# Masking a causal attention on GpSimd and normalising it by 32x32 transposes; two of four expert lists built inside the expert loop

## What is computed

```
scores = jnp.einsum('bhqd,bhkd->bhqk', q, k) / math.sqrt(float(dh))
scores = jnp.where(causal, scores, -jnp.inf)
attn = jax.nn.softmax(scores, axis=-1)
o = jnp.einsum('bhqk,bhkd->bhqd', attn, v)
return o.transpose(0, 2, 1, 3).reshape(B, S, D) @ W_o.T
```

## Time and profile before

| | us |
|---|---|
| median of 3 runs | 686.37 (685.69 to 686.54) |
| the profiled execution | 689.58 |
| its span | 687.5 |
| busy: PE, DVE, ACT, POOL | 468.5, 451.6, 318.3, 249.7 |
| TensorE weight loads (beside PE) | 299.1 |
| mean granted TensorE clock, of full speed | 0.764 |

### The profile page before, as it was taken

One profiled execution on the slowest core, in us unless ns is written; L12 is line 12 of the kernel. 1 busy time (PEld: TensorE's weight loads), 2 busy tenths in 40 slices (PEclk: granted clock), 3 DMA queues, 4 the chain that ended last, 5 costly groups with the idle time before them and its releaser, 6 DMA issues.

```text
span 687.5 us, 10676 instructions
## 1 busy us (share of the span) xinstructions
PE 468.5 (68%) x3820; PEld 299.1 (44%) x3820; DVE 451.6 (66%) x778; ACT 318.3 (46%) x550; POOL 249.7 (36%) x380
## 2 busy tenths in 40 slices
PE   3956816567887997867787888877858137556540
PEld 2525703353555775655343333433337126434330
DVE  5897999968495767477888897988835861101003
ACT  1343305534203442457888888898842103333320
POOL 5443479972800000430111111111101045888870
PEclk9987867968998999898555555566557557999995
DMA  8630000000000000001999999999995165895546
GB/s 309 182 131 1 0 0 1 1 0 0 2 1 2 2 2 2 1 1 35 184 177 178 180 179 186 174 183 184 186 176 190 40 203 142 218 199 110 90 68 193
DMA packets 170259, 70.73 MB, mean 103 GB/s; under 512 B 142240, under 2 KB 167776, under 8 KB 170208
## 3 DMA queue, kind: packets, MB, share of 16 engines
q1 hardware_dynamic: 164064, 61.15, 41.8%
q0 software_dynamic: 6144, 8.92, 7.5%
HBM read 27.56 MB, written 8.93 MB: 53 GB/s over the span
## 4 chain that ended last, share of the span: by engine, by line
PE 28%; DVE 23%; issue 17%; ACT 12%; DMA 11%; POOL 8%; POOLq 0%; SPq 0%; DVEq 0%; ACTq 0%
ACT KV L610 8%; PE ps L662 5%; DMA KV<-KV 5%; DVE AT L1167 4%; POOL b L484 3%; DMA A<-x_rows,slot_token 3%; PE ps L816 3%; POOL sums L505 2%; PE ps L848 2%; ACT A L594 2%; DMA sums<-A,slot_token 2%; POOL A L491 2%; PE ps L831 2%; PE ps L654 2%; PE ps L829 1%
## 5 line engine op out<-in xcount | busy, mean ns | idle before, releaser
L1237 DVE TENSOR_REDUCE nm<-ps 128x1 f32<-128x1024 f32 x128 | 154.3, 1223 | 27.3 <-PE ps L894 25.6
L610 ACT ACTIVATE KV<-ps,b,sq 128x1024 int16<-128x1024 f32 x128 | 153.3, 1201 | 29.2 <-POOL b L484 14.7
L894 PE MATMUL ps<-A 128*128 128x512 bf16 x256 | 125.0, 590 | 34.7 <-ACT KV L610 32.8
L484 POOL TENSOR_SCALAR b<-nm,sq 128x1 f32<-128x1 f32 x128 | 33.8, 264 | 174.4 <-DVE nm L1237 148.9
L903 PEld LDWEIGHTS ps<-VI,KV 128*128 128x128 f16 x1024 | 55.0, 113 | 74.3 <-issue 53.4
L1326 DVE TENSOR_TENSOR AT<-AT,ps 128x128 f32<-128x128 f32 x32 | 9.2, 288 | 86.7 <-ACT AT L632 86.7
L505 POOL DMA_INDIRECT sums<-A,slot_token x32 | 50.8, 1586 | 21.5 <-ACT A L639 12.1
L903 PE MATMUL ps<-VI,KV 128*128 128x16 f16 x1024 | 50.9, 179 | 7.7 <-DMA KV<-KV 7.6
L413 POOL TENSOR_SCALAR veps<-mv 128x4 f32<-128x4 f32 x12 | 3.0, 248 | 142.6 <-DVE mv L981 142.5
L491 POOL DMA_INDIRECT A<-x_rows,slot_token x32 | 34.8, 1089 | 37.7 <-issue 35.9
L517 ACT ACTIVATE XT<-ps 128x256 f32<-128x256 f32 x48 | 18.3, 386 | 55.8 <-PE ps L654 55.7
(11 more groups left out here) (271 smaller groups left out, 1001.4 us busy)
## 6 DMA issues: line engine op xcount, KB each, us to landing
A<-in SPq DMA_DIRECT2D x32, 256.0 KB, 3.6
A<-in SPq DMA_DIRECT2D x32, 128.0 KB, 4.0
A<-in SPq DMA_DIRECT2D x2, 1024.0 KB, 14.2
sums<-zeros SPq DMA_DIRECT2D x4, 512.0 KB, 5.3
KV<-KV SPq DMA_TRANSPOSE x128, 3.3
A<-sums SPq DMA_DIRECT2D x8, 256.0 KB, 4.7
X<-in SPq DMA_DIRECT2D x1, 1024.0 KB, 6.0
ctxT<-in SPq DMA_DIRECT2D x1, 1024.0 KB, 8.6
```

Of the source, the lines that this page charges most:

```text
L484: g.tensor_scalar(b5[:, n % 4:n % 4 + 1], nm5[:, n % 4:n % 4 + 1], sq5[:, q, h:h + 1], LN255, ALU.mult, ALU.add).then_inc(S["bias5_ready"], 1)
L610: a.activation(Y5[:, n % 4, :], ps[:, 2 * (n % 3):2 * (n % 3) + 2, :], ACT.Exp, scale=sq5[:, q, h:h + 1], bias=b5[:, n % 4:n % 4 + 1], acc ...
L894: done = T.matmul(ps[:, 2 * (n % 3) + c, :], QT5[:, h, q * P:(q + 1) * P], KT5[:, h, c * 512:(c + 1) * 512], start=True, stop=True)
L1237: v.tensor_reduce(nm5[:, n % 4:n % 4 + 1], ps[:, 2 * (n % 3):2 * (n % 3) + 2, :].rearrange("p a c -> p (a c)"), AX.X, ALU.max, negate=True ...
```

## The change

1. **Mask.** The mask matmul (L829), causalT, its memset and its select go. The first matmul into a bank now has start=True. After the exponential POOL sets the entries above the diagonal of two heads to 0 (affine_select over 128 x 2 x 256 elements, in place, one per half group, 32 in all); O(u) waits for this (mask4_ready) and no longer for the exponential. The selects stand in POOL's order after vint_ready and ahead of norm_rstd(4).
2. **Sums.** V4 gets a column of ones at position 16 of each head; the matmuls with ones go. The sum of a query then lies on partition 32r + 16 of the head.
3. **Normalisation.** DVE transposes the 128x256 outcome in blocks of 32x32 from PSUM to SBUF, takes the reciprocal of 128x8 sums, multiplies 128x8x16, and transposes back into QT4. The bank is free after the first transpose.
4. **Lists.** Lists 0 and 1 are built ahead of the loop. Lists 2 and 3 are cut into three pieces each, at steps s = 0, 3, 6 and s = 8, 11, 14 of DVE's loop, and 3, 6, 11, 14 of PE's.

```diff
+LIST_AT = [0, 0, 0, 8]
-        causalT = sb("causalT", [P, P], BF16)
...
-        r4 = XT[:, :, :].rearrange("p k c -> p (k c)")[:, 1536:2048].rearrange("p (i c) -> p i c", i=2)
+        OQ4 = XT[:, :, :].rearrange("p k c -> p (k c)")[:, 1536:2048].rearrange("p (i n c) -> p i n c", i=2, c=32)
+        ON4 = A[:, 15360:15872].rearrange("p (i n c) -> p i n c", i=2, c=32)
+        r4 = sb("r4", [P, 2, 8])
...
-            g.memset(V4[:, :, :, HD:2 * HD], 0.0).then_inc(S["v4_pads"], 1)
+            g.memset(V4[:, :, :, HD:HD + 1], 1.0).then_inc(S["v4_pads"], 1)
+            g.memset(V4[:, :, :, HD + 1:2 * HD], 0.0).then_inc(S["v4_pads"], 1)
...
+            for n in range(2 * G4):
+                pool.wait_ge(S["exp4_ready"], n + 1)
+                e = E4[n // 2 % 3][:, 2 * (n % 2):2 * (n % 2) + 2, 0:2 * P].rearrange("p j (a c) -> p j a c", a=2)
+                g.affine_select(out=e, in_=e, compare_op=ALU.is_ge, fill=0.0, base=0,
+                                pattern=[[0, 2], [0, 2], [1, P]], channel_multiplier=-1).then_inc(S["mask4_ready"], 1)
             norm_rstd(4)
...
                     for r in range(4):
-                        T.matmul(ps[:, banks[r], 0:SEQ], identb[:, :], causalT[:, :].unsqueeze(1).to_broadcast([P, 2, P]), start=True, stop=True)
-                    for r in range(4):
-                        T.matmul(ps[:, banks[r], P:P + SEQ], k0[r], q01[r], start=False, stop=True, skip_group_check=True)
-                    for r in range(4):
-                        last = T.matmul(ps[:, banks[r], 0:P], k1[r], q1[r], start=False, stop=True, skip_group_check=True)
+                        T.matmul(ps[:, SETS4[(2 * i + r // 2) % 3] + r % 2, P:P + SEQ], k0[r], q01[r], start=True, stop=True)
+                    for r in range(4):
+                        last = T.matmul(ps[:, SETS4[(2 * i + r // 2) % 3] + r % 2, 0:P], k1[r], q1[r], start=True, stop=True)
...
-                    pe.wait_ge(S["exp4_ready"], 2 * u + 2)
+                    pe.wait_ge(S["mask4_ready"], 2 * u + 2)
...
+            v.memset(ON4[:, :, :, HD:32], 0.0).then_inc(S["on4_zero"], 1)
...
-                v.reciprocal(r4[:, u % 2, :], ps[:, bank, SEQ:2 * SEQ]).then_inc(S["r4_ready"], 1)
+                oq, on, r = OQ4[:, u % 2, :, :], ON4[:, u % 2, :, :], r4[:, u % 2, :]
+                v.transpose(oq.rearrange("p n c -> p (n c)"), ps[:, bank, 0:SEQ]).then_inc(S["oq4_ready"], 1)
+                dve.wait_ge(S["oq4_ready"], u + 1)
+                v.reciprocal(r, oq[:, :, HD]).then_inc(S["r4_ready"], 1)
                 dve.wait_ge(S["r4_ready"], u + 1)
-                v.tensor_tensor(QT4[:, g, b * SEQ:(b + 1) * SEQ], ps[:, bank, 0:SEQ], r4[:, u % 2, :], ALU.mult).then_inc(S["on4_ready"], 1)
+                v.tensor_tensor(on[:, :, 0:HD], oq[:, :, 0:HD], r.unsqueeze(2).to_broadcast([P, 8, HD]), ALU.mult).then_inc(S["om4_ready"], 1)
+                dve.wait_ge(S["om4_ready"], u + 1)
+                v.transpose(QT4[:, g, b * SEQ:(b + 1) * SEQ], on.rearrange("p n c -> p (n c)")).then_inc(S["on4_ready"], 1)
...
-            for n in range(NE // EG):
+            for n in range(2):
                 onehots(n)
+                list_diagonal(n)
                 tokens(n)
             for s in range(NE):
...
+                for n in range(2, NE // EG):
+                    if s == LIST_AT[n]:
+                        onehots(n)
+                    if s == LIST_AT[n] + 3:
+                        list_diagonal(n)
+                    if s == LIST_AT[n] + 6:
+                        tokens(n)
```

More of the change, by code:

```diff
@@ L378, in _ @@
             g.memset(onesb[:, :], 1.0).then_inc(S["const_ready"], 1)
-            g.memset(causalT[:, :], 0.0).then_inc(S["const_ready"], 1)
-            pool.wait_ge(S["const_ready"], 8)
+            pool.wait_ge(S["const_ready"], 7)
             for m in (identf, identb):
@@ L845, in _ @@
                     wait_o4_bank(pe, slot)
-                    for lo, w in ((0, [V4[:, 2 * b:2 * b + 2, 4 * g + r, :] for r in range(4)]), (SEQ, [onesf[:, 0:64].rearrange("p (t c) -> p t c", t=2)] * 4)):
-                        for r in range(4):
-                            T.matmul(ps[32 * r:32 * r + 32, bank, lo:lo + SEQ], w[r][:, 0, :], e[:, r, P:P + SEQ], start=True, stop=False)
-                        for r in range(4):
-                            last = T.matmul(ps[32 * r:32 * r + 32, bank, lo + P:lo + SEQ], w[r][:, 1, :], e[:, r, 0:P], start=False, stop=True)
+                    for r in range(4):
+                        T.matmul(ps[32 * r:32 * r + 32, bank, 0:SEQ], V4[:, 2 * b, 4 * g + r, :], e[:, r, P:P + SEQ], start=True, stop=False)
+                    for r in range(4):
+                        last = T.matmul(ps[32 * r:32 * r + 32, bank, P:SEQ], V4[:, 2 * b + 1, 4 * g + r, :], e[:, r, 0:P], start=False, stop=True)
                     last.then_inc(S["o4_psum"], 1)
@@ L935, in _, with list_spread @@
                 last.then_inc(S["grid_psum"], 1)
+            def list_spread(n):
                 pe.wait_ge(S["diag_ready"], n + 1)
                 T.matmul(ps[:, 7, n * 64:(n + 1) * 64], spread6[:, :], diag6[:, n % 2, :, :].rearrange("p e c -> p (e c)"), start=True, stop=True).then_inc(S["list_psum"], 1)
+            pe.wait_ge(S["const6_ready"], 4)
+            for n in range(2):
+                list_grid(n)
+                list_spread(n)
             for s in range(NE + 2):
```

20 lines of the change are left out of this document (11 added, 9 removed).

## The result

| | before | after | difference |
|---|---|---|---|
| median of the runs, us | 686.45 (4 runs) | 667.06 (4 runs) | -19.4, predicted -25.2 |
| ratio, 95% interval | | 0.970 (0.962 to 0.977) | |
| profiled execution, us | 689.58 | 669.24 | -20.3 |
| its span | 687.5 | 667.5 | -20.0 |
| busy PE, DVE, ACT, POOL | 468.5, 451.6, 318.3, 249.7 | 446.4, 441.1, 317.8, 271.6 | -22.1, -10.5, -0.5, +21.9 |

The forecast was 661.2 (656.5 to 668.5): the sign and the range held, and the median lies 5.9 us above the forecast. The narrower range that the prediction gave for its own account, 657.5 to 666, missed by 1.1 us.

The account below looks back on a forecast made before the run. It took PE's matmuls to bound pass 2, and POOL's scatters, started by PE's first expert, to bound the end. Gains of 19.9 (pass 2) and 5.3 us (lists) took 686.4 to 661.2 us, range 656.5 to 668.5.

Parts of the forecast that it names:

- the 19.9 of pass 2: Pass 2: without mask and ones matmuls its end moves from 281.8 to 261.9 us, a gain of 19.9 us.
- the 5.3 of the lists: Expert lists: two fewer ahead of the loop, less a new wait for the first gather, gain 5.3 us.
- rival 4: Expert lists: the work moved in delays POOL as much, so they give nothing; 666.5 us, chance 7%.
- rival 1: Pass 2: POOL's selects are the bound; at 2.14 us each 689.3 us, slower by 0.4%; chance 10%.
- The pace of pass 2: Pass 2: S, ACT's start, the exponential and PE's restart set a step of 1.86 us, not PE's own 1.66.
- they cost nothing up to 1.36 us each: Pass 2, POOL: four steps and an out_proj give 10.9 us for 8 selects, hiding up to 1.36 us each.
- I let it fall again: Early pass 2: PE's clock falls to 1.2 GHz at about 213 us and rises at 219.8, as before.
- the 5.2 us for the last out_proj: End of pass 2: the last out_proj takes 5.2 us, chosen between 3.65 and 6.71 at the low clock.
- Rival 2: Pass 2: PE's clock does not hold; 7 + 5 us are given back, 673 us; chance 8%.
- S(0) at 210.35 as now: Start of pass 2: the first S comes at 210.35 us, unchanged from the kernel before.
- The second memset in V4: Ahead of pass 2, POOL: the added memset is hidden, its results being wanted over 100 us later.
- rival 3: Pass 2, DVE: transpositions are slow; at 1.76 us each 692 us, slower; chance 5%.

Follow-up runs that it names:

- run 6: Changed kernel with masks by POOL's selects but the old normalisation (sums by matmuls with ones, reciprocal of 128x256 from PSUM): 677.35 us.
- run 7: Changed kernel with sums by V4 and normalisation by transpositions, but masks still written by matmuls: 674.92 us.
- run 9: Changed kernel with each select on POOL followed by one over half of its elements again: 669.26 us.
- run 8: Changed kernel with each select on POOL done twice in a row, with a wait between: 676.97 us.
- run 2: Changed kernel with the constant causalT made as before (one memset and one select more on POOL), though nothing reads it: 666.46 us.
- run 5: The kernel before the change once more, unaltered: 687.66 us, ratio 1.004 against other executions of the same kernel.
- run 4: Kernel before with only lists 2 and 3 moved into the expert loop, pass 2 and constants as before: 681.81 us, ratio 0.995.
- run 3: Changed kernel without its lists, all four built ahead of the expert loop as before: 671.08 us, ratio 0.979.
- run 10: Changed kernel with SP issuing the weights of experts 8 to 15 only after the first gather has landed: 665.00 us, ratio 0.973.

## Why the prediction was right, and where it was off

The two mechanisms that it named did what it said, and both terms of the sum can be found in the traces: 16.7 us at equal clock for the 19.9 of pass 2, and 5.6 for the 5.3 of the lists. The range held partly by luck: 667.06 is over the 666 up to which the forecast's own account went, and lies in the stated range only because that was widened for rival 4 and mild forms of rival 1, neither of which happened.

**The pace of pass 2: right.** The prediction put a step at 1.86 us, set by S, ACT's start, the exponential and PE's restart; it was 1.91, with PE waiting 0.19 for ACT. From S(4) to S(15) it had 30.8 us, and the trace 255.88 - 224.64 = 31.2. Runs 6 and 7 show that it is this loop: with the mask left on PE the step is 2.45, over PE's 2.20.

**The selects: cost right, slack wrong.** 0.69 us against 0.85 taken, and hidden but for 1.0 us at the last group. The sentence "they cost nothing up to 1.36 us each" failed. The tail may grow, which its range allowed for; but ahead of the tail, too, 0.8 us of the 1.3 were lost at 1.07 us a half group (run 9), and 5.2 of the 6.3 at 1.41, where the same average with the measured times would let POOL just keep up (run 8). It divided four steps and an out_proj by eight selects. In the middle of the pass that is nearly so (12.0 us a batch for 11.3 of selects). But the first out_proj comes only behind the seventh S, and until then POOL must keep the pace of a step, 1.91 / 2 = 0.95 us, or use up its lead of two groups; and in each batch it idles 0.76 us, since it can't work further ahead than S and the exponentials have got.

**DVE: right.** 0.445 us a transposition against 0.42 taken; a group 1.50 us from its first start to its last end (226.43 to 227.93) against 1.42, under the step of 1.91. The Trainium skill, "VectorE: DVE Perf Modes", section "The three transpose paths", led to an estimate of 0.62 us for this size. The trace does not agree: it is 0.445.

**Low clock in pass 2: wrong both ways.** The step "I let it fall again" cost the forecast 2.0 us (S(0) to S(4) 9.65 against 7.65 measured), and the 5.2 us for the last out_proj 1.7 (it took 3.5 until the keys started). Against that the tail and the steps were 0.7 longer. So the stretch came out 2.9 us shorter than forecast, 48.6 against 51.5. Rival 2 (the clock doesn't hold) did not come; PE waited 0.19 us in each step at 1.00. The Trainium skill, "TensorE: Matmul & The Clock Gate", section "A second HAM failure mode: psum-queue depth-cycling", had made it likely. None of the seven profiles with this pass 2 unaltered shows it: a granted clock of 1.00 in all of it, 48.6 to 49.0 us each.

**The base of the sum: the largest error.** The term of 19.9 us was 281.8 less 261.9, read against one profiled execution. That execution had its own luck with the clock: 5.6 us more in pass 2 than the two others of the same code, and a start of pass 2 at 210.35 where the others began at 213.80 and 207.69. At equal clock the gain in pass 2 is 16.7 us, 3.2 less than the term. The subtraction was right for that execution (22.7 measured, since the clock then did better than assumed) but not for the median of many. What lies ahead of pass 2 was taken to stay: "S(0) at 210.35 as now". It came at 216.99, and in no profile of the changed pass before 213.97.

**The second memset in V4: wrong, by all that the rows show.** The prediction held it hidden, "since POOL's results of that part are wanted over 100 us later". Its own results are, but DVE works beside it. Before the change and after it, the timeline of DVE:

```profile
92.72 4.00 DVE L988 TENSOR_SCALAR XN<-X,mv,rstd 128x256 f32<-128x256 f32 x4 [0.28 <-POOL rstd L415]
...
99.41 0.27 DVE L1090 TENSOR_SCALAR dq<-am,w 128x8 f32<-128x8 f32 x1
99.59 0.16 DVE L1092 TENSOR_SCALAR qs<-qs 128x8 f32<-128x8 f32 x1
```

```profile
92.71 4.29 DVE L1001 TENSOR_SCALAR XN<-X,mv,rstd 128x256 f32<-128x256 f32 x4 [0.28 <-POOL rstd L413]
...
99.80 0.59 DVE L1103 TENSOR_SCALAR dq<-am,w 128x8 f32<-128x8 f32 x1
100.31 0.16 DVE L1105 TENSOR_SCALAR qs<-qs 128x8 f32<-128x8 f32 x1
```

DVE's four passes beside the memsets take 4.29 us for 4.00 (the first alone 2.87 for 1.87, the others less than before), and behind them one small instruction takes 0.59 for 0.27. DVE reaches L1105 0.7 us later, and PE's first matmul of the feed-forward network comes as much later behind the same DVE pass in run 2 than in run 5. All three profiles with one memset have 4.00 (runs 4 and 5 and the first), and all eleven with two have 4.28 or 4.29 and 0.59 or 0.60. From the start of the first memset to DVE's L1092 or its counterpart pass 6.94 to 6.96 us in the three and 7.67 to 7.69 in the eleven, with the constants as before (run 2) or the lists as before (run 3) too. The Trainium skill, "SBUF — State Buffer", section "SBUF: two separate sides", says that POOL and some of DVE's instructions shut each other out for whole instructions rather than share. That would give steps of this kind, and no run here takes it apart. That the split of the memset is the cause is read from these rows; no run puts the single memset back alone.

**What stays open.** In three profiles with the old memset the first S of pass 2 comes at 207.69 to 213.80, in all eleven with the new at 213.97 to 217.16. Means are 4.8 us apart: 0.8 are there already when that memset starts (90.4 to 92.7 us in the three, 91.1 to 93.4 in the eleven); 0.7 are the memset's; 1.3 come in the feed-forward network up to V's projection; and 2.0 from there on. The constants are excluded (run 2). The last part is one level of the clock: V's projection took 4.64 us in two of the three old profiles and 7.19 in the third, and 7.19 in all eleven new ones. So the old kernel shows that chance plays a part, and that none of the eleven is at the high level speaks for a lasting cost as well; these runs don't settle it, and no run has the new pass 2 with the single memset.

**The lists: right.** 5.3 us forecast, 6.1 less 0.45 = 5.6 in the first pair, 5.85 in run 4. The new wait is the one named: PE starts the loop at the first gather's landing, 6.5 us behind its issue against 6.0 taken (5.4 in run 4), and run 10 shows that it is behind the weights. POOL's pace stayed 3.27 us a scatter. List 3's digits cost one scatter 0.6 us (2.17 against 1.59, at 572.91), against 0.5 forecast; the loop as a whole grew by 0.45 to 1.0 us in the profiles of the unaltered change and run 2. Rival 4 (no gain) is excluded by runs 3 and 4 in their stages, rivals 1 and 3 by selects of 0.69 and transpositions of 0.445 us.

In sum: 16.7 for pass 2 and 5.6 for the lists make 22.3 us at equal clock. The medians give 18.1 to 19.3, so 3 to 4 us are lost elsewhere: 0.7 at the memset, and the rest ahead of pass 2, where it is open how much is the change's and how much chance. Forecast: 25.2, of which 3.2 were in the base of pass 2.

## What to carry to other kernels

Before a gain is read against one profiled execution, look at the granted clock of every stage that goes into the subtraction, and take the work at equal clock: here the same code took 71.3 us in one profile and 65.6 in two others. Where engines pass work on through a few buffers, an average over a batch with a pause in it overstates an engine's slack, above all before the first pause: there it has the time of one step and its lead. And an instruction that nobody waits for need not be free while it runs beside an engine on the path.

## What was not expected of the hardware

- TensorE's granted clock decides more than most edits here: 5.6 us in one pass, 2.6 us in V's projection (4.64 or 7.19 for the same sixteen matmuls, in the same kernel). Idles of 1.13 and 2.73 us ahead of the last out_proj were followed by 3.69 us at 2.4 GHz in run 5, and idles of 1.13 and 2.74 by 5.33 us, partly at 1.2 GHz, in run 6: the idle alone does not decide it.
- A select on POOL costs 284 ns for 128 elements, 0.41 us for 256 and 0.64 us for 512 (run 9, the most frequent values): by these three about 0.15 us and 1 ns an element, far under the 1071 ns that the same engine's TENSOR_SCALAR takes for 256.
- A block transposition of 128x256 f32 on DVE takes 445 ns from SBUF and 444 from PSUM, near the multiplication of the same size, 424 ns.
- A gather of rows of 288 f32 for 128 partitions lands 3.8 us behind its issue, or 5.4 to 6.7 us when the weights of eight experts were issued just ahead. With the weights held back the loop took 0.8 to 1.4 us longer than the changed kernel's.
- A POOL scatter issued beside DVE's f16 comparisons took 2.17 us to issue instead of 1.59 (at 572.91).
